# A DLRM-style pair-product MLP on one core: five raw weight buffers, tile-by-tile start, a new placement of all side work

## What is computed

```python
sparse_embed = emb_tables[field_idx[None, :], x_sparse]
z = sparse_embed.reshape(B, N_FIELDS * K)
gram = jnp.einsum('bik,bjk->bij', sparse_embed, sparse_embed)
inner = gram[:, iu, ju]
dnn_in = jnp.concatenate([x_dense, z, inner], axis=-1)
h = jax.nn.relu(dnn_in @ w1 + b1)
out = jax.nn.sigmoid(h @ w2 + b2)
```

## Time and profile before

| | |
|---|---|
| median of three runs | 447.29 us |
| profiled execution: first to last instruction | 584.9 us |
| profiled execution's own time | not given apart from its span |
| PE busy | 436.1 us, 75% |
| DVE / ACT / POOL busy | 316.2 / 274.3 / 215.9 us |
| data read from memory | 77.55 MB, 133 GB/s over the span |

### The profile page before, as it was taken

One profiled execution on the slowest core, in us unless ns is written; L12 is line 12 of the kernel. 1 busy time (PEld: TensorE's weight loads), 2 busy tenths in 40 slices (PEclk: granted clock), 3 DMA queues, 4 the chain that ended last, 5 costly groups with the idle time before them and its releaser, 6 DMA issues.

```text
span 584.9 us, 6070 instructions
## 1 busy us (share of the span) xinstructions
PE 436.1 (75%) x2011; PEld 355.6 (61%) x2011; DVE 316.2 (54%) x670; ACT 274.3 (47%) x443; POOL 215.9 (37%) x215
## 2 busy tenths in 40 slices
PE   7814040999787899445999932059989999999997
PEld 7613030777675777334887721047867888887885
DVE  4510010565638698302679830049886478989542
ACT  2400020383689867315986630029543368864330
POOL 6777772477723437770005777700000000000000
PEclk9967575899999999755999975568989999999999
DMA  7643351569634857441356863312666373465730
GB/s 232 154 71 62 26 98 12 155 160 277 189 78 117 201 156 226 85 61 34 113 156 206 214 153 26 62 36 62 152 206 219 102 244 106 141 193 196 258 90 0
DMA packets 29455, 77.96 MB, mean 133 GB/s; under 512 B 8480, under 2 KB 8488, under 8 KB 29424
## 3 DMA queue, kind: packets, MB, share of 16 engines
q1 hardware_dynamic: 22768, 70.75, 38.8%
q0 software_dynamic: 6656, 6.83, 11.4%
HBM read 77.55 MB, written 0.00 MB: 133 GB/s over the span
## 4 chain that ended last, share of the span: by engine, by line
PE 42%; another core or an unknown queue 18%; ACT 15%; issue 12%; DVE 9%; DMA 2%; SPq 1%; POOL 1%; DVEq 0%; ACTq 0%
PE ps L562 13%; PE ps L574 12%; PE ps L564 12%; ACT w_hi L627 4%; DVE w_lo L733 3%; ACT gram L662 3%; DVE weighed L837 2%; PE ps L522 2%; ACT pair_u L648 2%; ACT pair_v L651 2%; PE ps L508 2%; DMA w_raw<-in_L_rec_w_dram 1%; ACT pair_v L650 1%; SPq L392 1%
## 5 line engine op out<-in xcount | busy, mean ns | idle before, releaser
L451 POOL DMA_INDIRECT z<-in_L_rec_emb_tables_dram,idx x208 | 214.9, 1033 | 162.6 <-PE ps L508 99.4
L562 PE MATMUL ps<-w_hi,x_hi 128*128 128x502 f32 (+1 forms) x512 | 212.5, 415 | 73.2 <-issue 46.5
L564 PE MATMUL ps<-w_lo,x_hi 128*128 128x502 f32 (+1 forms) x480 | 194.0, 404 | 4.6 <-issue 4.6
L733 DVE TENSOR_TENSOR w_lo<-w_raw,w_hi 128x1002 fp32r<-128x1002 f32 x120 | 141.2, 1200 | 100.8 <-ACT w_hi L627 51.6
L627 ACT CAST w_hi<-w_raw 128x1002 fp32r<-128x1002 f32 x128 | 128.7, 1033 | 83.6 <-remote 27.7
L562 PEld LDWEIGHTS ps<-w_hi,x_hi 128*128 128x128 f32 x512 | 101.1, 197 | 102.9 <-issue 55.6
L574 PE MATMUL ps<-w_hi,x_lo 128*128 128x502 f32 (+1 forms) x480 | 142.8, 403 | 4.0 <-issue 3.1
L564 PEld LDWEIGHTS ps<-w_lo,x_hi 128*128 128x128 f32 x480 | 95.1, 198 | 21.4 <-issue 4.2
L574 PEld LDWEIGHTS ps<-w_hi,x_lo 128*128 128x128 f32 x480 | 92.8, 196 | 23.9 <-issue 4.3
L635 ACT CAST x_hi<-ps 128x256 fp32r<-128x256 f32 (+2 forms) x36 | 16.2, 472 | 121.6 <-PE ps L508 62.2
L662 ACT COPY gram<-ps 32x104 f32<-32x104 f32 x160 | 39.7, 248 | 54.3 <-remote 32.7
(11 more groups left out here) (46 smaller groups left out, 184.4 us busy)
## 6 DMA issues: line engine op xcount, KB each, us to landing
w_raw<-in_L_rec_w_dram SPq DMA_DIRECT2D x112, 501.0 KB
w_raw<-in_L_rec_w_dram SPq DMA_DIRECT2D x24, 250.5 KB
w_raw<-in_L_rec_w_dram SPq DMA_DIRECT2D x8, 438.4 KB
z<-in_L_rec_emb_tables_dram,idx POOLq DMA_INDIRECT x208
w_raw<-in_L_rec_w_dram SPq DMA_DIRECT2D x24, 62.6 KB
w2b<-in_L_rec_w_dram SPq DMA_DIRECT2D x1, 501.0 KB
w2b<-in_L_rec_w_dram SPq DMA_DIRECT2D x1, 500.0 KB
w_raw<-in_L_rec_w_dram SPq DMA_DIRECT2D x8, 50.9 KB
```

The source lines that it names most:

```text
L451: pool.indirect_dma_start(out=z[:, t % 2, K * f:K * (f + 1)], out_offset=None, in_=emb_rows, in_offset=bass.IndirectOffsetOnAxis(ap=idx[:, ...
L562: nc.tensor.matmul(into(c, t), hi, of_w(w_hi, c, k), start=first, stop=False)
L564: nc.tensor.matmul(into(c, t), hi, of_w(w_lo, c, k), start=False, stop=False)
L733: nc.vector.tensor_tensor(low, raw(n)[at, :], high, ALU.subtract).then_inc(w_lo_done, 1)
```

## The change

The diff, cut to its core:

```diff
-    JOINT = [[(0, 1), (1, 1), (2, 1), (3, 1), (4, 1), (5, 1), (6, 1), (7, 1), (8, 1), (9, 1), (10, 1), (11, 1), (12, 1)], [(0, 2), (2, 2), (4, 2), (6, 2), (8, 2), (10, 2), (12, 1)]]
+    ALONE = 2
+    BOTH = tuple(range(GROUP))
+    JOINT = [[(k, 1, (b,)) for k in range(ALONE) for b in BOTH] + [(k, 1, BOTH) for k in range(ALONE, FP)],
+             [(0, 2, BOTH), (2, 2, BOTH), (4, 2, BOTH), (6, 2, BOTH), (8, 2, BOTH), (10, 2, BOTH), (12, 1, BOTH)]]
+    ACROSS = SIDES * FIELDS
-    WARM_UP = 36
+    WARM_UP = 29
     PLAN = {
-        ('J', 0): [-1.0, 0.0, 3.0, 4.0, 6.8, 8.5, 10.8, 12.5, 14.8, 16.5, 18.0, 19.8, 22.8],
+        ('J', 0): [-1.0, -0.5, 0.0, 1.0, 2.0, 4.0, 6.4, 8.5, 10.8, 12.5, 14.3, 15.7, 18.0, 19.8, 22.5],
-        ('O', 0): [14.3, 23.9],
+        ('O', 0): [17.7, 23.7],
-        ('O', 1): [27.6, 29.1],
+        ('O', 1): [28.2, 29.3],
-        ('G', 1): [30.5, 31.5, 31.5, 31.6, 31.7, 31.7, 33.0, 33.0],
+        ('G', 1): [29.8, 30.4, 30.5, 30.6, 31.5, 32.9, 33.1, 33.2],
-        ('X', 0): [33.5],
+        ('X', 0): [29.6],
-        ('T', 4): [52.5, 52.5, 52.6, 53.0],
+        ('T', 4): [38.4, 50.7, 51.3, 53.3],
-        ('T', 6): [84.5, 84.5, 84.5, 89.0],
+        ('T', 6): [70.5, 81.1, 84.9, 85.6],
-        ('T', 7): [81.8, 81.8, 81.8, 81.8],
+        ('T', 7): [70.9, 76.3, 77.7, 89.2],
...
     }
-    WARM = [(2.9, 6), (5.2, 1), (33.3, 4), (34.4, 4), (39.7, 6)]
+    WARM = []
-    RAW = 4
+    RAW = 5
-        pair_v = sb("pair_v", [P, APART // 2, SIDES, QUAD, 2], f32r)
+        pair_v = sb("pair_v", [P, APART // 2, SIDES, FIELDS, 2], f32r)
-            return [m for m in range(2, PIECES) if max(PIECE[m][0] - LEAD, turns_before(m) - 1, 0) == u]
+            return [m for m in range(2, PIECES) if max(PIECE[m][0] - LEAD, turns_before(m) - 1, FIRST) == u]
-            load(0)
+            for n in range(RAW):
+                if n >= HALVES:
+                    sp.wait_ge(w_lo_done, n - HALVES + 1)
+                load(n)
             sp.dma_start(idx[:, GROUP:TILES, :], by_tile[:, GROUP:TILES, :]).then_inc(idx_rest, 16)
-            for n in range(1, 6):
-                load(n)
+            load(RAW)
-                        bank(("G", t, q))[:, P * g:P * (g + 1)],
+                        bank(("G", t, q))[:, ACROSS * g:ACROSS * (g + 1)],
+                if only is not None:
+                    for c in cs:
+                        high_parts(c, only, ks[0])
+                        last = low_part(c, only, ks[0])
+            later = [second_alone(k) for k in range(ALONE)]
             for u in range(FIRST, TURNS):
-                if u >= 0:
+                if 0 <= u < HALVES * ALONE:
+                    if u % HALVES == 0:
+                        multiply(u, 0)
+                        transpose_z(second_alone(u // HALVES))
+                        multiply(u + 1, 0)
+                    multiply(u, 1)
+                elif u >= 0:
                     multiply(u)
                 for kind, t, q in between(u):
-                    PARTS[kind](t, q)
+                    if (kind, t, q) not in later:
+                        PARTS[kind](t, q)
```

More of the change, by code:

```diff
@@ L81, in product_interaction_mlp_kernel @@
         for h in range(HALVES):
-            split = pair == 1 and h == 0
+            split = (pair, h) in SPLIT
             for k in range(FP if split else KT):
@@ L219, in slices_of @@
         if kind == "J":
-            first, n = JOINT[t][q]
-            return [(GROUP * t + b, k) for b in range(GROUP) for k in range(first, first + n)]
+            first, n, of = JOINT[t][q]
+            return [(GROUP * t + b, k) for b in of for k in range(first, first + n)]
         first, n = BATCHES[q]
@@ L226, in slices_event @@
         if t < GROUP * EARLY_PAIRS:
-            return next(("J", t // GROUP, q) for q, (first, n) in enumerate(JOINT[t // GROUP]) if first <= k < first + n)
+            return next(("J", t // GROUP, q) for q, (first, n, of) in enumerate(JOINT[t // GROUP])
+                        if first <= k < first + n and t % GROUP in of)
         return next(("T", t, q) for q, (first, n) in enumerate(BATCHES) if first <= k < first + n)
@@ L459, in _ @@
                     pool.wait_ge(idx_done, 2)
-                for q, (first, n) in enumerate(JOINT[pair]):
+                for q, (first, n, of) in enumerate(JOINT[pair]):
                     if pair:
-                        pool.wait_ge(transposed, count("JTX", slices_event(GROUP * (pair - 1), first + n - 1)))
+                        pool.wait_ge(transposed, count("JTX", slices_event(GROUP * pair - 1, first + n - 1)))
                     for k in range(first, first + n):
-                        for b in range(GROUP):
+                        for b in of:
                             gather(GROUP * pair + b, k, gathered_j[q])
@@ L675, in keep_z_part @@
                 sum_ended(act, s)
[L676 to L677 removed]
+                if kept_last(t, c) is not None:
+                    act.wait_ge(weighed_done, SUMS.index(kept_last(t, c)) + 1)
                 nc.scalar.copy(zpart[:, kept(t, c), 0:WIDTH[c]], ps[SEAT[s]][:, 0:WIDTH[c]]
@@ L751, in pair_operands @@
                 for par in range(2):
-                    at = QUAD // 2 * par + first
-                    for pairs, x in ((pair_u, x_lo), (pair_v, x_hi))[0:1 if t in ACT_COPIES else 2]:
+                    at, to = QUAD // 2 * par + first, FP * par + first
+                    for pairs, x, at in ((pair_u, x_lo, at), (pair_v, x_hi, to))[0:1 if t in ACT_COPIES else 2]:
                         last = nc.vector.tensor_copy(
@@ L846, in _ @@
             split_piece(0)
-            for pairs in (pair_u, pair_v):
-                pads = pairs[:].bitcast(fp32).rearrange("p a s (r k) b -> p (a s) r (k b)", r=2)
-                last = nc.vector.memset(pads[:, :, :, 2 * FP:], 0.0)
-            last.then_inc(pad_zero, 1)
             split_piece(1)
-            make_rows(slice(GROUP, TILES), idx_rest, 3)
             for u in range(FIRST, TURNS):
```

111 lines of the change are left out of this document (61 added, 50 removed).

## The result

| | before | after |
|---|---|---|
| median, 22 executions each, same chip | 449.37 us (445.17 to 453.55) | 448.56 us (443.24 to 455.83, and one at 1015.67) |
| ratio after to before | | 0.9943, 95% interval 0.9916 to 0.997 |
| profiled execution | 584.9 us span, and 446.8 in a second one | 455.95 us, of which 454.1 are the span |

The ratio leaves out every execution more than 1.5% above the fastest of its kernel, and the changed kernel has more of those (9 of 22, before 4), so over all executions the medians differ by 0.2% alone, and how much of the ratio's gain a user would see is open. By the ratio the gain is 0.6%, 2.6 us of 449.4, just above the 0.5% that can be told from nothing; the forecast was 7.9. On 447.29 the ratio gives 444.7, inside the range, but the measured 448.56 lies above its upper end of 446.

A forecast was written before the change was run, and what follows sets the result against it. PE was taken as the bound, except turns 24 to 33, paced by ACT, and the start, waiting for gathers. Gains 5.0 + 2.4 + 0 + 0 + 0.5 = 7.9 us took 447.3 to 439.4 us; range 432 to 446.

The forecast's parts named there:

- The start, 5.0 us: Turns 0 to 3: turn 0 needs two gathers instead of four, so turn 4 starts near 24.7 instead of 30.0; 5.0 us gained.
- The bound of 2.5: Turns 0 to 3: if gathers land 2.5 us later among reordered w loads, 2.5 us of the start's gain remains.
- WARM_UP 29: Before turn 0: 7 matmuls fewer in a run that ends before the first gather lands; worth nothing.
- Fillers, 2.4 us: Later fillers, after the start: removing them saves PE their time, 0.2 + 0.9 + 1.3; 2.4 us gained, bounds 0 and 3.3.
- The rival about the clock: Likeliest behind the wait in turn 3: without fillers the clock falls to 1.2 GHz, kernel slower, 450.8 us; chance 0.06.
- Width of pair_v: Pair products on PE: 104 instead of 128 streamed columns gain 0, since the weight load is the full side.
- the bound of 5.6: Pair products on PE: if time went with streamed columns, 256 products would save 5.6 us in all.
- A fifth raw buffer: Loads of w: one can start a piece earlier, but PE hardly ever stood for w; slack, 0 to 1.
- The late part: PE's idle time from 388 us on and from 270 to 338: new places win 0.5 us, bounds -1 and +3.
- The middle: Turns 24 to 33, where ACT sets the pace: new places can return some or add; 0, bounds -3 and +4.
- T4's batch before turn 39: In front of turn 39: gather 110 lands 3 to 4 us before PE needs it; 0, bound 5.1 lost.
- gathers swallow it: In front of turn 39: at 1.41 us a gather PE waits 5.1 us for gather 110; 444.5 us, chance 0.20.

The follow-up runs named there:

- half-lookup runs: Every second lookup of pair 1 left out (26 gathers): in the changed kernel 0.9828, in it with the start in pairs 0.9932, in the kernel before 0.9985.
- experiment 4: The new start alone (tile by tile, w one by one, early splits, 29 warm-up matmuls) in the kernel before, four buffers, old places: 1.0051.
- experiment 5: All 21 fillers removed from the kernel before, nothing else changed: 1.0077.
- experiment 7: Kernel before with the new places alone: 1.0073; changed kernel with four raw buffers: 1.0021; changed kernel with four buffers and wide pair_v: 1.013.

## Why the prediction was wrong

Too much was gained on paper, and the terms that made the sum were not the ones that made the gain. Step by step:

**The start, 5.0 us: failed; 0 measured (0.5% slower alone).** Three numbers were off. Before, turn 4 really begins at 28.1, not 30.0, as the first profile had it: 1.9 (the wait of 1.02 at 21.29 isn't in the second). The twelfth gather was expected to be asked for at 18.71 and is at 19.87: 1.2. It was expected 4.36 us after that, and comes after 6.3: 2.0. Together 5.1, the whole of the term. The step that failed is "its twelfth gather is asked for at 18.71 and lands 4.36 later": one landing time stood for all. Before, this gather took 2.4 us, so the kernel before couldn't show the wait; by all that the profiles show it comes with the new requests for w. The bound of 2.5, gathers landing 2.5 us later because the reordered w loads fall among them, had the mechanism and was the nearer one. A second step failed too: "WARM_UP 29 takes 7 matmuls off a run that ends before the first gather lands". The run ends at 11.4, 2.9 us after both gathers of turn 0 have landed, and it is why turn 0 begins as late as 12.40 instead of near 10.7. And even a start that is faster is passed on only if the next thing is. The half-lookup runs point to the gathers of pair 1: 4.7 us between the two starts with 26 gathers fewer, none with all of them.

**Fillers, 2.4 us: failed, with the wrong sign; -3.5 us alone.** The price of 0.113 us a record was right, and it was taken for the whole effect. The argument "PE idled 11.1 us in pieces and the granted clock stayed at 1.00" used a trace in which the fillers were there. A trace can't show what an instruction prevents while it is in place. Its other half, "after the long stalls alone it was at the lower one", was a misreading: the same trace has PEclk 0.50 from 428.5 to 431.9, 37 us after the last stall. The rival about the clock had 0.06 and looked at the start. There nothing happened in the changed kernel; in experiment 4, the start alone, it did. In experiment 5 its place is turns 33 to 41.

**Width of pair_v: 0 on PE was right** (118 ns in both), with 0.6 to 1.1 us of the bound of 5.6 by the means. The rule of the Trainium skill (TensorE: Matmul & The Clock Gate, LDWEIGHTS (loading the stationary operand)), that a load's time goes by the stationary operand's columns, gave an estimate of 2.6 at most, and the traces agree: with 104 streamed columns a load still lasts 201 ns on average, with 128 it lasts 198. What was missed is on ACT: its work was called "the same in number and size". It is the same in number of elements, and 0.11 us longer per write at the other row length. Alone, the narrow pair_v costs 0.65%, 2.9 us. With the new places and four buffers it gains 1.1% instead (experiment 7), for a reason that no run shows.

**A fifth raw buffer, "slack, 0 to 1": failed, and without it the change gains nothing;** 4.8 us in the kernel before, and 0.9943 against 1.0021 in the changed kernel, 3.5 us. The reason given was that PE hardly ever stood for w in the dense stretches. PE doesn't wait for w_raw in any profile; ACT does, for 43.3 us in the second profile of before (39.6 with the narrow pair_v), and what PE waits for is probably the work queued behind that wait. One more look, at ACT's waits, would have shown it.

**The late part, 0.5: right in sign and size;** turns 74 to 120 take 0.8 us less in both profiles of the changed kernel. **The middle, 0, bounds -3 and +4: mis-sized.** All new places alone, with the fillers kept, cost 0.73%, 3.3 us (1.7 to 4.9). That "the new places can return some or add to it" was right, and alone they add: in that profile turns 24 to 33 are 4.5 us longer.

**T4's batch before turn 39, 0: nearly right, in part by luck.** No wait stands there in the first profile of the changed kernel. In the second, on PE's timeline, there is one of 0.73:

```profile
161.41 0.55 PE L524 MATMUL ps<-ident,z 128*128 128x128 f32 x3 [0.73 <-DMA z<-in_L_rec_emb_tables_dram,idx]
```

The margin of 3 to 4 us wasn't there. The gathers came some 8 us later than the 153.0 forecast, and PE came to this place later as well (160.7 in that profile, 156.8 forecast).

**The rival "gathers swallow it", 444.5 at 0.20, was nearest.** Its pace of 1.41 us a gather is the measured one (1.416), and its gain of 2.8 us is near the measured 2.6. That the number fits so well is luck: it still books 2.4 us for the fillers and nothing for the buffer. Its place was wrong, in front of turn 39; most of the waits are in turns 24 to 33, in front of pair 1's transposes. The forecast took 1.327 instead, from the profile with stalls, in which many gathers ran while less data moved (DMA share 0.36 to 0.38). Over the 92 gathers that turn 33 needs, the difference is 92 x 0.089 = 8.2 us, and the forecast never asked whether turn 33's were there in time.

What I expected to see: turn 0 near 10.7 (12.40), turn 4 near 24.7 (27.84), waits for gathers under 1 us before turn 39 (12.1 and 6.0 in the two profiles); no fillers and unchanged pitch held.

The terms measured one by one don't add up to the whole. Start +0.5%, fillers +0.8% (six of them are missing in the start's run too), places +0.7%, width +0.65% and buffer -1.1% would make the change 1.6% slower, and the ratio is 0.6% faster. Put together in steps it looks like this: the first three add up to +2.0% alone and to +1.3% together (the wide kernel with four buffers, 0.8 to 1.8); narrowing pair_v then takes 1.1% off, where alone it adds 0.65; the fifth buffer takes off 0.8%. So most of the gap is the width, whose sign turns with the places. Why is open. Also open: what makes executions of the changed kernel differ by 12 us. Its first profile, one of the long ones, has 8 us more in turn 33, behind a late gather, and 3.6 in turns 57 to 73 (but 3.0 less in 41 to 56). A run that asks for pair 1's gathers some us earlier would test the first, and wasn't made.

## What to carry to other kernels

Before a profile with stalls is used, see which engines went on in them: what is read there about who is ahead of whom may be false, and a second profile is worth having. A buffer is judged by the waits of the engine that reads it and by what is queued behind them, not by the bottleneck's own waits. Take out work that "does nothing" only with a run of its own, since the trace that holds it can't show what it prevents. Don't add up parts that were measured alone: here their sum is 2.2% off. When requests for data are put in another order, ask which other requests they now fall among; and follow a gain at the start to the next engine that paces the kernel before it is booked.

## What was not expected of the hardware

- The first profiled execution of before was 138 us longer than the second, in three stretches in which PE, ACT and DVE nearly stood and POOL's gathers went on. One timed execution of the changed kernel took 1015.67 us. Neither has an explanation here.
- A gather's issue takes 0.94 us in two of three cases (137 of 208 in the changed kernel) and up to 2.5 us in the others, with no wait that the profile shows; this alone lifts the pace from 1.25 to 1.41 us. The data came 6.3 us after the request for the twelfth, 8.0 for the 92nd and 4.36 for the fourth of before; recorded landings in one trace of the changed kernel go from 2.4 to 8.6.
- Behind waits of 2.58 us (experiment 4, at 15.58) and 5.92 (changed kernel, at 142.03) the clock was at 1.2 GHz for 3.4 and 9 us, though PE was busy for most of the time around them; behind the 2.35 at 26.20 it stayed full. The 21 fillers were worth 0.8%.
- A pair product keeps its median of 118 ns at 104 and at 128 columns, and takes 213 to 214 at half the clock.
- ScalarE writes the same 64x896 elements in 1018 ns into rows of 32 fields and in 1130 into rows of 26.
